# New order of the side items over the half steps of a four-stage image chain, with new bank tables, new waits and another order of loads

## What is computed

```python
# L0: per channel a 32x32 attention between rows
Q, K, V = conv1x1(x, Wq), conv1x1(x, Wk), conv1x1(x, Wv)       # 128 channels
y = conv1x1(softmax(Q @ K.T) @ V, Wr)
x = batchnorm(y) + x
# L1: 8 heads of attention over the 1024 pixels
q, k, v = split(w_qkv @ group_norm(x, 32))
x = x + w_proj @ (softmax(q.T @ k) applied to v)
# L2: linear attention
k, v = split(kv_w @ group_norm(x, 16)); q = softmax(k, channels); k = softmax(k, pixels)
x = xn + out_w @ gelu(group_norm(context(k, v) @ q, 16))
# L3: upsample by 2 (12-tap FIR, both axes), leaky ReLU, downsample by 2
```

## Time and profile before

| | |
|---|---|
| median of three runs | 4220.44 us (4216.12 to 4232.14) |
| the profiled execution | 4221.9 us, span 4219.9 us |
| TensorE busy | 3713.0 us, 88% |
| VectorE, ScalarE busy | 2883.6 us (68%), 2979.6 us (71%) |
| mean granted clock of TensorE | 0.938 of 2.4 GHz |

### The profile page before, as it was taken

One profiled execution on the slowest core, in us unless ns is written; L12 is line 12 of the kernel. 1 busy time (PEld: TensorE's weight loads), 2 busy tenths in 40 slices (PEclk: granted clock), 3 DMA queues, 4 the chain that ended last, 5 costly groups with the idle time before them and its releaser, 6 DMA issues.

```text
span 4219.9 us, 72611 instructions
## 1 busy us (share of the span) xinstructions
PE 3713.0 (88%) x22401; PEld 1815.3 (43%) x22401; DVE 2883.6 (68%) x5019; ACT 2979.6 (71%) x6992; POOL 41.3 (1%) x57
## 2 busy tenths in 40 slices
PE   4989899898988989899899988989898898989876
PEld 2444445354453535445353443535445353444422
DVE  3667677777767776777677767767676777777653
ACT  1877777777777777767777777777777777777831
POOL 0000000000000000000000000000000000000000
PEclk7889999999999999999999999999999999999896
DMA  2112120211211012120111212011121111211000
GB/s 70 53 36 56 36 64 7 56 44 41 61 34 56 17 41 59 36 65 16 51 41 38 61 36 64 7 46 54 36 66 28 40 40 39 62 36 53 7 14 10
DMA packets 75656, 177.19 MB, mean 42 GB/s; under 512 B 16352, under 2 KB 19040, under 8 KB 73184
## 3 DMA queue, kind: packets, MB, share of 16 engines
q1 hardware_dynamic: 75232, 171.95, 15.0%
HBM read 36.62 MB, written 17.30 MB: 13 GB/s over the span
## 4 chain that ended last, share of the span: by engine, by line
PE 57%; DVE 17%; issue 13%; ACT 11%; SPq 1%; DVEq 1%; ACTq 0%; DMA 0%; POOL 0%; POOLq 0%
PE ps L1065 22%; PE ps L1130 8%; PE ps L1093 7%; PE ps L1109 7%; DVE mxh L655 5%; ACT ps L959 4%; PE ps L1517 3%; DVE st L537 2%; ACT prob L950 2%; PE ps L1567 2%; PE ps L1549 2%; PE ps L1576 1%; PE ps L1559 1%; ACT u L1021 1%; PE ps L1452 1%
## 5 line engine op out<-in xcount | busy, mean ns | idle before, releaser
L959 ACT ACTIVATE ps<-ps,mxh 128x512 f32<-128x512 f32 x2048 | 1366.3, 675 | 456.0 <-DVE mxh L655 433.1
L655 DVE TENSOR_REDUCE mxh<-ps 128x1 f32<-128x512 f32 x2048 | 1310.4, 680 | 365.1 <-PE ps L1109 357.3
L950 ACT ACTIVATE prob<-ps 128x512 f32<-128x512 f32 x2048 | 1124.1, 612 | 424.4 <-PE ps L1093 421.7
L1093 PE MATMUL ps<-qs,ks 97*128 97x512 f32 x2048 | 912.9, 525 | 92.3 <-ACT prob L950 64.0
L1109 PE MATMUL ps<-ks,qs 96*128 96x512 f32 x2048 | 727.4, 424 | 99.1 <-ACT ps L959 77.3
L1093 PEld LDWEIGHTS ps<-qs,ks 97*128 97x128 f32 x2048 | 364.4, 197 | 599.2 <-issue 376.3
L1130 PE MATMUL ps<-prob,vo 128*32 128x512 f32 x4096 | 582.1, 642 | 0.0
L1109 PEld LDWEIGHTS ps<-ks,qs 96*128 96x128 f32 x2048 | 404.4, 198 | 280.8 <-ACT ps L959 179.3
L959 ACT ACTIVATION_READ_ACCUMULATOR ps<-ps,mxh 128x1 f32 x2048 | 444.2, 217 | 0.0
L1065 PE MATMUL ps<-xn,wqk 128*128 128x512 f32 x512 | 280.0, 680 | 3.9 <-DVE xn L582 3.9
L638 DVE SCALAR_TENSOR_TENSOR lo<-ps,vec,hi 128x512 fp32r<-128x512 f32 x128 | 96.1, 751 | 244.7 <-ACT hi L985 244.7
(11 more groups left out here) (121 smaller groups left out, 3622.7 us busy)
## 6 DMA issues: line engine op xcount, KB each, us to landing
qs<-hi SPq DMA_DIRECT2D x256, 128.0 KB, 2.4
ks<-hi SPq DMA_DIRECT2D x256, 128.0 KB, 2.3
xb<-in_x SPq DMA_DIRECT2D x32, 512.0 KB, 4.2
qs<-lo SPq DMA_DIRECT2D x128, 128.0 KB, 2.4
ks<-lo SPq DMA_DIRECT2D x128, 128.0 KB, 2.3
xa<-xb SPq DMA_DIRECT2D x16, 1024.0 KB, 4.6
recs<-recd SPq DMA_DIRECT2D x64, 256.0 KB
out<-xn SPq DMA_DIRECT2D x32, 512.0 KB, 2.6
```

What stands on the lines that cost most here:

```text
L655: dve.tensor_reduce(mxh[:, k, e:e + 1], ps[:, MAX_BANKS[at % 3], :], AX_X, ALU.max, negate=True).then_inc(max_ok.sem, 1)
L950: act.activation(prob[:, n % 2, h, :], ps[:, k % 2, :], ACT.Exp).then_inc(p_ok.sem, 1)
L959: act.activation(ps[:, bank, :], ps[:, bank, :], ACT.Exp, bias=mxh[:, k, e:e + 1], accum_out=sumh[:, m // NT % 2, k, e:e + 1]).then_inc(su ...
L1093: pe.matmul(ps[:, k % 2, :], ks[0:STACK + 1, (u // 2) * Q4 + h, s * P:(s + 1) * P], qs[0:STACK + 1, u, h, :], start=True, stop=True).then_ ...
```

## The change

**Tables.** `SIDE` is written anew: the same items, in other half steps and partly in another order. `BANK` follows it, and so do the waits of `bank_free`. At one place the two tables read:

```diff
-    36: ["norm1a", "stats3b"], 37: ["norm1b"], 38: ["norm3a", "q0a"], 39: ["q0b", "k0a"], 40: ["k0b", "norm3b"],
-    41: ["v0a", "gelu"], 42: ["v0b"], 43: ["z0a", "z0b"], 44: ["z1a"], 45: ["turn3", "z1b", "zt0"],
+    36: ["rows2", "norm1a"], 37: ["norm1b", "o21b"], 38: ["stats3b", "q0a", "q0b"], 39: ["norm3a", "k0a"],
+    40: ["norm3b", "k0b", "gelu", "v0a"], 41: ["v0b", "z0a"], 42: ["z0b"], 44: ["zt0", "turn3", "z1a", "z1b"],
```

**The end.** It has an order (`TAIL`) and banks (`TAIL_BANK`) of its own, over all eight banks, which nothing else uses by then:

```diff
+TAIL = ( ... "z0a", "z0b", "zt0", "z1a", "z1b",
+    "wu00", "wu01", "hu00", "hu01", "zt1", "leaky00", "hu02", "wu10", "leaky01", "hu03", "leaky02", "wu11", "hd00a",
+    "hd00b", "hu10", "leaky03", "hd01a", "leaky10", "hu11", "hd01b", "hu12", "leaky11", "hu13", "leaky12", "wd0a",
+    "leaky13", "wd0b", "hd10a", "hd10b", "hd11a", "hd11b", "wd1a", "wd1b",
+)
+def bank_of(name, i):
+    return TAIL_BANK[name] if i == B - 1 else BANK.get(name, 6)
```

**Waits.** Three waits on all of a group become waits on the part that is read, and one is added:

```diff
-                if ct == 0 and m == 0:
-                    pe.wait_ge(ke_ok.sem, ke_ok(i, 2))
+                if ct == 0:
+                    pe.wait_ge(ke_ok.sem, ke_ok(i, m + 1))
...
-                if m == 0 and hf == 0:
-                    pe.wait_ge(qn_ok.sem, qn_ok(i, NT))
+                if m == 0:
+                    pe.wait_ge(qn_ok.sem, qn_ok(i, 4 * hf + 4))
...
-                if ct == 0 and hf == 0:
-                    pe.wait_ge(qc_ok.sem, qc_ok(i, 4))
+                if ct == 0:
+                    pe.wait_ge(qc_ok.sem, qc_ok(i, 3 + hf))
...
+                dve.wait_ge(kv_ok.sem, kv_ok(i, NT * m + NT))   # q_maxima
```

```diff
+                load(0)
+                for dst, src in early:
+                    sp.dma_start(dst[...], src).then_inc(early_in.sem, 16)
                 for made in looped:
                     sp.sem_inc(made.sem, START)
+                sp.sem_inc(started.sem, 1)
...
+            def stack_keys():
+                act.wait_ge(lo1_ok.sem, lo1_ok(0, 4))
+                act.wait_ge(hi1_ok.sem, hi1_ok(0, 4))
+                for h in range(Q4):
+                    for r, of in enumerate((hi1, hi1, lo1)):
+                        act.dma_start(ks[DH * r:DH * r + DH, h, :].bitcast(F32), ...)
```

More of the change, by code:

```diff
@@ L443, in last @@
             def last(i):
-                for names in SIDE.values():
-                    for name in names:
-                        if not name.startswith(OF_B + OF_J) and name != "copy_x":
-                            side(name, None, i, None)
+                for name in TAIL:
+                    side(name, None, i, None)
             periods(sp, first, period, last)
@@ L485, in last @@
             def last(i):
-                for names in SIDE.values():
-                    for name in names:
-                        if not name.startswith(OF_B + OF_J):
-                            side(name, None, i, None)
+                for name in TAIL:
+                    side(name, None, i, None)
             periods(pool, first, period, last)
@@ L1244, in bank_free @@
                     else:
+                        pe.wait_ge(cmc_ok.sem, cmc_ok(i, 1))
+                elif name == "l0vb":
+                    if b is None:
+                        pe.wait_ge(l0_sb.sem, l0_sb(j, 4))
+                    elif b is not None and i is None:
+                        pe.wait_ge(l0_sb.sem, l0_sb(j, 4))
+                    else:
                         pe.wait_ge(cmb_ok.sem, cmb_ok(i, 1))
+                elif name == "corr0":
+                    pe.wait_ge(l0_sb.sem, l0_sb(j, 5))
                 elif name == "corr1":
```

604 lines of the change are left out of this document (390 added, 214 removed), and 50 rows, old and new, of tables (BANK, SIDE, TAIL, TAIL_BANK).

## The result

The changed kernel takes 3866.55 us, median of four runs (3858.72 to 3871.74); the kernel before, in the same session, 4222.15. The ratio is 0.916, 95% interval 0.9144 to 0.9176: 356 us less, where 266 were forecast.

The account below looks back on a forecast made before the run. TensorE was taken as the bound, with 34 us a pass lost around it. Fourteen passes at 14 us, 12 for first and last pass, 20 start and 38 end make 266 off 4221.9: 3956 us, range 3880 to 4075.

Parts of the forecast that it names:

- group norm of L2, beginning of the pass: Loop, half steps 3 to 8: earlier statistics, with key products as cover, win 2.5 of 3.7 us a pass.
- L0, contexts, `av`: Loop, half steps 20 to 33: finer waits, new order and separate banks win 5 us a pass, bounds 0 and 9.
- group norm of L1: Loop, half steps 34 to 39: later `stats3b` and `o21b` in half step 37 win 5.5 of 6.4 us a pass.
- gelu: Loop, gelu moved to half step 40: TensorE has enough work while ScalarE is away; 3.0 of 3.5 us a pass.
- L3 and the turn: Loop, half steps 45 to 0: more even `hd` and `wd`, empty first half step; 2.5 us a pass.
- Costs: Loop: empty half steps 23 and 43 lose 2.6, `turn3` on a shared bank 0.6, stacking DMAs 1.3; 4.5 us a pass.
- end: After the loop: eight banks and mixed channel tiles in L3, contexts and other items win 38 us, bounds 28 and 44.
- start: Before the loop: earlier begin 12.5, separate banks 4, keys on ScalarE's queue 3.6; 20 us, bounds 14 to 23.
- the DMA wall: Rival: half step 44 waits for the stacked keys, taking 4 of the 14 us a pass; 4012 us, chance 0.12.
- light and heavy half steps: Rival: empty or nearly empty half steps go at ScalarE's pace, half the loop's gain remains; 4060 us, chance 0.12.
- the slower case: Rival: in half steps 20 to 33 some 30 us of TensorE's work runs at 1.2 GHz; 4306 us, chance 0.03.
- All of it: Rival: no new costs, L0's part gives 9 us a pass, start and end their best; 3831 us, chance 0.06.

Follow-up runs that it names:

- c1_corr: The changed kernel with `corr0` moved from half step 21 to 20, ahead of `flipv`, so a core stands between it and `corr1`; 3837.8 us.
- f1_fill: The changed kernel with empty half steps filled: `proj1a` moved from 3 to 4, `ctx0b` from 22 to 23, `z0b` from 42 to 43; 3845.0 us.
- e1_two: The changed kernel with the end's new order kept, but in banks 6 and 7 only instead of eight; 3894.4 us.

## Why the prediction was wrong in size

The direction was right by far. The loop has 77 of the missing 90 us. Its forecast, net of the costs in the half steps where they fall, beside the two ways of measuring (us a pass; "by place" is the difference of the losses in the table of half steps):

| part | forecast | by place | undone |
|---|---|---|---|
| group norm of L2, beginning of the pass | 2.5 | 2.5 | 3.1 |
| L0, contexts, `av` | 5 - 1.3 = 3.7 | 4.5 | 8.5 |
| group norm of L1 | 5.5 | 7.4 | 5.3 |
| gelu | 3.0 - 1.3 = 1.7 | 3.6 | 1.8 |
| L3 and the turn | 2.5 - 0.6 - 1.3 = 0.6 | 1.1 | 1.5 |
| sum | 14.0 | 19.1 | 20.2 |

- *L0's softmax, contexts and `av`*. **This is the step that failed**: "I take 5, a little over the middle, because the share of it that hangs on VectorE is spread over four half steps more". That priced the part by the idle time in its own half steps, and the group norm behind it as if it stood alone. For its own half steps the size was not bad (3.7, and 4.5 by place, 2.9 when undone). But undone, the part costs 8.5 us a pass, because 5.2 of loss come back in half steps 34 to 39. 3.1 of the 8.5 is a wait on one shared bank with the clock behind it; the text named the separate banks and gave them no price of their own, though the waits of 0.75 and 1.92 stood in the trace. 1.0 is the earlier statistics of L1. How the rest of the old middle part delays the group norm stays open. The 8.5 is net of a loss that the change added: "`corr0` and `corr1` stand together" was listed among its gains, and it is what made the pause in `corr1`, 2.2 us a pass by c1_corr.
- *Group norm of L1*: 5.5, undone 5.3, and by the named cause. The agreement is partly luck: by place 7.4 went, and this part alone doesn't cure the stall. Undoing the middle part, with the group norm as changed, brings 5.2 of it back.
- *Costs*: 4.5 were subtracted, and the runs show at most 1.9 of it. Of the 2.6 for two empty half steps, f1_fill shows 0.7 and 1.2 by place, and 1.0 once what the next half steps take back is counted. The 2.44 - 1.1 each took ScalarE's pace as if both engines entered the half step level (no row has the 1.1; the prediction's own bare core is 0.93). My reading, not shown by a run of its own: behind half steps 22 and 42, which hold products, TensorE enters late, and part of ScalarE's longer time only lets it catch up. The 1.3 for the DMAs isn't paid in the loop: the wall is touched and not hit. No run shows the 0.6 for `turn3`.
- *Gelu*: the wait of 3.5 was read rightly and is nearly gone.
- *Group norm of L2, L3 and the turn*: the gross 2.5 for L3 was too high; the clock there is not better than before (6.6 us low for 4.4).

By undoing, the middle is 4.8 too low, L3 with its costs 0.9, the beginning of the pass 0.6, the gelu 0.1, the group norm 0.2 too high: 6.2, of which 0.7 is overlap between the parts; 5.5 a pass remain, 77 us. By place the largest shares are the group norm and the gelu, 1.9 each. Both say the same: the parts were priced one at a time, and too much was subtracted.

First and last pass give 3.1 more than forecast, the *end* 11.3 more (49.3 for 38, above its bound of 44): L3 28.8 of 30, contexts and transposes 7.2 of 5 (in its bounds), but the other stretches 13.3 where I had 3. 10.6 of it are the `kv`, `o2` and `z` stretches; I had read and priced only those of the earlier trace rows. Their gain doesn't come from the banks: e1_two, in two banks, has 9.9 of it. The *start* was right within 1.3: begin 13.0 earlier (12.5), banks and order 4.2 (4), keys 1.8 (3.6), 18.7 in all (20).

The rivals: the DMA wall exists, but about 1 us further on; light and heavy half steps cost 1.0, and not half of the gain; the clock did fall in one place of half steps 20 to 33, for 6.1 us a pass, far from the 30 us of work that the slower case needed. The Trainium skill's rule on a clock that oscillates with short idle times between groups (TensorE: Matmul & The Clock Gate, "A second HAM failure mode: psum-queue depth-cycling") is borne out only so far that the lower level followed a pause of 0.51 to 1.12 us in the middle of tiny products; in half steps 34 to 43, with waits of 0.5, the clock stays at 2.4 GHz. "All of it" (3831) was the nearest number and had 0.06.
